# Degree count of a graph kernel: 98-wide high one-hots, and the low keys of eight split five to three between VectorE and ScalarE

## The chip, the cores and the metric

The kernel runs on one core of one Trainium2 chip. The metric is the time of one execution on the device, in microseconds, lower being better; the time shown is the median of three runs.

## The reference

Two message-passing layers with a layernorm after each, over 12,500 nodes of 128 features and 200,000 edges whose destinations are sorted. The part that matters here is the first step, the degree of every node (how many edges end in it), which the first layer needs for its edge weights:

```python
src, dst = (edge_index[0], edge_index[1])
mask = (src != dst).astype(x.dtype)
deg = jax.ops.segment_sum(mask, dst, num_segments=N) + 1.0
dinv = deg ** (-0.5)
edge_w = dinv[src] * dinv[dst] * mask
...
h = x @ W1 + b1
h = spmm(h)          # sum over edges of h[src] * edge_w, by dst
...
```

The second layer is an attention over the same edges with eight heads. None of the rest is touched by the change.

## The kernel before

Node number n is split in two: its node tile (n >> 7, of which there are NT = 98) is the high key, its row in the tile (n & 127) the low key. The 200,000 edges lie as 128 partitions (P) by 1568 columns. A stage is a block in which each engine runs its own instruction list, with semaphores between them; the stages run one after another. The order is: load of keys and constants, `count_destinations`, `find_bases`, then the first layer and so on.

`count_destinations` (the class `Degrees`) makes a table of 98 node tiles by 128 rows out of matmuls. For one column of 128 edges, the one-hot of the high key (an edge per partition, a node tile per column) is the stationary operand, and a row of the low key is the moving one, so that the product adds each edge to its cell. PSUM (`bank[0]` and `bank[1]`) accumulates over all 1568 columns. The columns are taken in halves of HALF = 8; two halves make a turn of TURN = 16, and there are 98 turns, so 196 halves. Per half:

- GpSimd (`stage`) copies the eight columns of both keys in three small copies: two to bf16 (L401), one in f32 (L402). It has four half-sized buffers and may run that far ahead.
- VectorE (`vector_half`) writes `highs` for all eight columns in one `tensor_tensor` (L408): 128 rows by 8 keys, 1024 elements per partition. Then it writes `lows` for the keys of `BY_VECTOR`, four of the eight, in a second one (L411): 128 rows by 4 keys, 512 elements.
- ScalarE (`scalar_half`) makes the other four, `BY_SCALAR`, one `activation` each (L418): the sign of (row + 0.5 - key), 128 elements. The sign form is a running count that the next stage differences again.
- TensorE (`tensor_half`) runs eight matmuls of 128 stationary by 129 moving columns (the last one counts all edges): four with `lows` into `bank[1]` (L430), four with `signs` into `bank[0]` (L434).

`highs`, `lows` and `signs` each have two half-sized buffers: VectorE and ScalarE may write a half once TensorE has used the half two before it. In SBUF `highs` is laid out [row, key], the key innermost, so that one key's stationary operand is read at a step of 8 elements (16 bytes); one key's `lows` are read at a step of 4 elements (8 bytes); `signs` are contiguous. A second class, `CountUpto`, does a like count beside the first layer; its one-hots are 98 wide and have 8 keys innermost, and its matmul is L518:

```python
self.highs = tmp("highs", [P, 2, NT, HALF], BF16)
self.upto = tmp("upto", [P, 2, P, HALF], BF16)
...
counted = nc.tensor.matmul(bank[0][0:NT, 0:P], self.highs[:, h, :, j], self.upto[:, h, :, j], start=False, stop=False)
```

In a profile the stationary operand's load stands as LDWEIGHTS on PEld and the product as MATMUL on PE. L778, L788 and L808 are matmuls of the second layer's sort that the rows below show; L808 moves `hot_hi`, 98 columns at a step of 16 bytes, L778 and L788 move contiguous bf16.

Of the kernel before, what the change touches and what calls it, by code (L numbers as in the profile page):

```python
# [5 lines left out]
F32, I32, BF16, U16 = mybir.dt.float32, mybir.dt.int32, mybir.dt.bfloat16, mybir.dt.uint16  # L6
ALU, ACT, AX = mybir.AluOpType, mybir.ActivationFunctionType, mybir.AxisListType

P = 128
# [3 lines left out]
NT = -(-N_NODES // P)  # L13
LAST_ROWS = N_NODES - (NT - 1) * P
PAD_NODE = NT * P - 1
HALF = 8
# [40 lines left out]
def need(eng, sem, value):  # L57

    if isinstance(value, int) and value <= 0:
        return  # L60
    eng.wait_ge(sem, value)
# [31 lines left out]
def gnn(nc, x, src, dst, attr, w1, b1, w2, b2, gamma, beta, bn_mean, bn_var,  # L93
# [14 lines left out]
    with whole:  # L108
        def sb(name, shape, dt=F32):
            return whole.enter_context(nc.sbuf_tensor(name, shape, dt))  # L110

        bank = [whole.enter_context(nc.psum_tensor(f"bank{i}", [P, 512], F32)) for i in range(8)]
# [5 lines left out]
        iota_rows = sb("iota_rows", [P, P, HALF], BF16)  # L118
# [6 lines left out]
        zeros_bf = sb("zeros_bf", [P, P + 1], BF16)  # L125
# [86 lines left out]
        with ExitStack() as ph:  # L212
            sem = ph.enter_context(phase_semaphores(nc))
            tmp = lambda n, s, d=F32: ph.enter_context(nc.sbuf_tensor(n, s, d))
# [160 lines left out]
        class Degrees:  # L375


            BY_VECTOR, BY_SCALAR = (0, 1, 2, 3), (4, 5, 6, 7)

            def __init__(self, sem, tmp):  # L380
                self.highs_ready, self.lows_ready, self.signs_ready, self.used, self.keys_ready, self.ones_ready, self.go = (
                    sem(n) for n in ("highs_ready", "lows_ready", "signs_ready", "hot_used", "keys_ready", "ones_ready", "go"))
                by_vector, by_scalar = len(self.BY_VECTOR), len(self.BY_SCALAR)
                self.highs = tmp("highs", [P, 2, P, HALF], BF16)
                self.lows = tmp("lows", [P, 2, P + 2, by_vector], BF16)
                self.signs = tmp("signs", [P, 2, by_scalar, P + 2], BF16)
                self.keys_bf, self.keys = tmp("keys_bf", [P, 4, 2, HALF], BF16), tmp("keys", [P, 4, HALF])
# [16 lines left out]
            def vector_half(self, dve, i, b, h):  # L404
                v = nc.vector
                need(dve, self.used, (i - 1) * TURN + (h + 1) * HALF)
                dve.wait_ge(self.keys_ready, (2 * i + h + 1) * 3)
                v.tensor_tensor(self.highs[:, h, :, :], iota_rows[:, :, :], self.keys_bf[:, 2 * b + h, 0, :].unsqueeze(1).to_broadcast([P, P, HALF]),  # L408
                                ALU.is_equal).then_inc(self.highs_ready, 1)
                some = len(self.BY_VECTOR)  # L410
                v.tensor_tensor(self.lows[:, h, 0:P, :], iota_rows[:, :, 0:some], self.keys_bf[:, 2 * b + h, 1, 0:some].unsqueeze(1).to_broadcast([P, P, some]),  # L411
                                ALU.is_equal).then_inc(self.lows_ready, 1)
# [7 lines left out]
            def zeros(self, **at):  # L420

                for n in range(2):
                    nc.tensor.matmul(bank[n][:, 0:P + 1], zeros_bf[:, 0:P], zeros_bf[:, :], **at)

            def tensor_half(self, pe, i, h):
                half = 2 * i + h
                pe.wait_ge(self.highs_ready, half + 1)
                pe.wait_ge(self.lows_ready, half + 1)
                for j in self.BY_VECTOR:
                    nc.tensor.matmul(bank[1][:, 0:P + 1], self.highs[:, h, :, j], self.lows[:, h, 0:P + 1, j],  # L430
                                     start=False, stop=False).then_inc(self.used, 1)
                for n, j in enumerate(self.BY_SCALAR):
                    pe.wait_ge(self.signs_ready, half * len(self.BY_SCALAR) + n + 1)
                    nc.tensor.matmul(bank[0][:, 0:P + 1], self.highs[:, h, :, j], self.signs[:, h, n, 0:P + 1],  # L434
                                     start=False, stop=False).then_inc(self.used, 1)

        class Count:
# [1309 lines left out]
        with ExitStack() as ph:  # L1747
            own = ph.enter_context(phase_semaphores(nc))
            sem = lambda n: own(f"qkv_{n}")
            tmp = lambda n, s, d=F32: ph.enter_context(nc.sbuf_tensor(f"qkv_{n}", s, d))  # L1750
# [104 lines left out]
        with ExitStack() as ph:  # L1855
            own = ph.enter_context(phase_semaphores(nc))
            sem = lambda n: own(f"expand_{n}")
            tmp = lambda n, s, d=F32: ph.enter_context(nc.sbuf_tensor(f"expand_{n}", s, d))
# [143 lines left out]
        with ExitStack() as ph:  # L2002
            own = ph.enter_context(phase_semaphores(nc))
            sem = lambda n: own(f"score_{n}")
            tmp = lambda n, s, d=F32: ph.enter_context(nc.sbuf_tensor(f"score_{n}", s, d))
# [226 lines left out]
        with ExitStack() as ph:  # L2232
            own = ph.enter_context(phase_semaphores(nc))
            sem = lambda n: own(f"soft_{n}")
            tmp = lambda n, s, d=F32: ph.enter_context(nc.sbuf_tensor(f"soft_{n}", s, d))
# [6 lines left out]
            BY_VECTOR = CHUNK_LEN * 3 // 4  # L2242
# [62 lines left out]
        with ExitStack() as ph:  # L2305
            own = ph.enter_context(phase_semaphores(nc))
            sem = lambda n: own(f"mix_{n}")
            tmp = lambda n, s, d=F32: ph.enter_context(nc.sbuf_tensor(f"mix_{n}", s, d))
# [143 lines left out]
        with ExitStack() as ph:  # L2452
            own = ph.enter_context(phase_semaphores(nc))
            sem = lambda n: own(f"fin_{n}")
            tmp = lambda n, s, d=F32: ph.enter_context(nc.sbuf_tensor(f"fin_{n}", s, d))
# [112 lines left out]
```

## Time and profile before

| what | value |
|---|---|
| median of 3 runs | 9340.04 us |
| lowest and highest | 9331.43, 9343.38 us |
| the profiled execution: time | 9334.91 us |
| the profiled execution: span | 9333.3 us |
| granted TensorE clock, mean | 0.796 of full |
| `count_destinations` in that span | about 51 to 284 us |

The span is from the first to the last instruction of the one profiled execution; the 1.6 us between span and time lie outside it. The stage that the change touches is 2.5% of the span, so a tenth of its length is 0.25% of the time. Busy time is the union of an engine's instructions; where instructions of one engine overlap, as ScalarE's and TensorE's do, the mean duration of one is longer than the time that each adds.

### The profile page before, as it was taken

Reading aid. Unit: us, or ns where it says so; the run is one execution under the profiler, and the core shown is the slowest. Engines: PE = TensorE matmul, PEld = TensorE weight load, DVE = VectorE, ACT = ScalarE, POOL = GpSimd, SP = SyncE. Lnnn points to the kernel's source line nnn. Section 1 sums busy time; section 2 is a strip of 40 time slices with the busy share of each in tenths; the row PEclk is TensorE's granted clock in tenths of the full one; section 3 lists DMA queues with packets and bytes.
Section 4 is the critical chain, followed back from the end, with each engine's and each line's share of the span. In section 5 each row is a group of like instructions: output and inputs, shape, how many; then the busy total and the mean of one; then the engine's idle time right before and its main releaser. Section 6 shows DMA issues by size and latency. Waiting matters only on the chain. (4 is left out here: it accounts for less than half of the span.)

```text
span 9333.3 us, 196145 instructions
## 1 busy us (share of the span) xinstructions
PE 6708.6 (72%) x37588; PEld 5384.7 (58%) x37589; DVE 5772.2 (62%) x15905; ACT 2627.6 (28%) x9043; POOL 6065.1 (65%) x6650
## 2 busy tenths in 40 slices
PE   6688888888677777777777646666666658854774
PEld 5556565656466766666666524444444447754663
DVE  7544444445466666666666565555555558888887
ACT  7311111111223333333333110000000025535884
POOL 6477777777655555555555657777777767744665
PEclk8688888898667677767677677878878789987997
DMA  1233333344321111111111133333333356643663
GB/s 45 57 105 107 107 106 108 108 110 109 94 75 42 42 42 42 42 41 41 40 40 39 46 98 114 114 113 114 114 113 114 114 156 167 168 107 103 165 164 96
DMA packets 1043673, 868.47 MB, mean 93 GB/s; under 512 B 188168, under 2 KB 936312, under 8 KB 1043624
## 3 DMA queue, kind: packets, MB, share of 16 engines
q0 software_dynamic: 179664, 437.87, 15.3%
q1 hardware_dynamic: 643032, 319.49, 13.1%
q10 hardware_dynamic: 220928, 110.57, 4.1%
q8 instruction: 16, 0.26, 0.0%
q14 instruction: 33, 0.27, 0.0%
HBM read 578.04 MB, written 287.84 MB: 93 GB/s over the span
## 5 line engine op out<-in xcount | busy, mean ns | idle before, releaser
L1561 POOL DMA_INDIRECT spmm_rows<-h_table,spmm_index_ring x3136 | 3120.1, 995 | 1738.7 <-issue 862.8
L1640 PE MATMUL bank<-spmm_rows,spmm_hot 128*128 x6660 | 1808.6, 365 | 145.5 <-SPq L1536 94.8
L1919 POOL DMA_INDIRECT kv_sorted<-expand_payload,expand_where_ring x1568 | 1503.5, 959 | 498.4 <-issue 398.3
L1640 PEld LDWEIGHTS bank<-spmm_rows,spmm_hot 128*128 128x128 f32 x6660 | 1404.2, 253 | 584.3 <-issue 564.2
L1612 DVE TENSOR_TENSOR region_ab<-region_ab,bank 128x128 f32 x3330 | 957.0, 287 | 1204.8 <-PE bank L1640 808.4
L1940 PE MATMUL bank<-region_ab,expand_hot_t 128*128 x3336 | 1117.2, 493 | 733.7 <-DVE expand_hot_t L1957 732.9
L1974 DVE SCALAR_TENSOR_TENSOR expand_payload<-expand_payload,region_c,bank 128x256 f32 x1668 | 801.1, 480 | 878.4 <-SPq L1881 620.2
L1940 PEld LDWEIGHTS bank<-region_ab,expand_hot_t 128*128 128x128 f32 x3336 | 765.5, 240 | 942.7 <-issue 817.1
L845 ACT COPY spmm_beside_next_slot<-bank 128x98 f32<-128x98 f32 x1568 | 377.6, 241 | 1903.3 <-PE bank L808 1895.8
L808 PE MATMUL bank<-spmm_beside_hot_hi,spmm_beside_hot_lo 128*128 128x98 bf16 x1568 | 556.3, 355 | 481.6 <-issue 481.6
L518 PE MATMUL bank<-spmm_beside_upto,spmm_beside_highs 128*98 128x128 bf16 x1568 | 686.3, 438 | 254.8 <-issue 252.0
L816 PE MATMUL bank<-spmm_beside_next_slot,spmm_beside_lo_t 128*128 128x98 f32 x3136 | 833.9, 361 | 0.0
L816 PEld LDWEIGHTS bank<-spmm_beside_next_slot,spmm_beside_lo_t 128*128 128x128 f32 x3136 | 738.3, 282 | 28.4
L767 DVE CUSTOM_DVE_ANT_0 spmm_beside_junk<-bank,spmm_beside_hot_hi 128x98 f32<-128x98 f32 x1568 | 450.2, 324 | 485.9 <-PE bank L817 485.9
L2111 POOL TENSOR_TENSOR score_terms<-score_q_sb,score_k_rows 128x512 f32<-128x512 f32 x420 | 528.8, 1269 | 240.0 <-ACT score_q_sb L2059 207.3
L2443 PE MATMUL bank<-mix_mixed,mix_hot 128*128 128x136 f32 x3360 | 489.6, 298 | 174.3 <-DVE region_ab L2407 161.9
L640 ACT COPY spmm_beside_attr_t<-bank 128x512 f32<-128x512 f32 x392 | 229.4, 585 | 1343.1 <-PE bank L679 1340.8
L1591 DVE TENSOR_TENSOR spmm_hot<-iota_bf,lo_slots 128x512 f32<-128x512 bf16 x834 | 576.9, 692 | 20.5 <-issue 20.5
L2346 POOL TENSOR_TENSOR mix_mixed<-mix_mixed 128x512 f32<-128x512 f32 x420 | 436.4, 1060 | 233.2 <-ACT mix_mixed L2361 152.0
L2443 PEld LDWEIGHTS bank<-mix_mixed,mix_hot 128*128 128x128 f32 x3360 | 437.7, 190 | 227.9 <-DVE region_ab L2407 200.7
L518 PEld LDWEIGHTS bank<-spmm_beside_upto,spmm_beside_highs 128*98 128x98 bf16 x1568 | 407.0, 260 | 274.7 <-issue 271.3
L817 PE MATMUL bank<-spmm_beside_hot_hi,spmm_beside_earlier 128*128 128x98 bf16 x1568 | 550.0, 351 | 0.0
(358 smaller groups left out, 11797.0 us busy)
## 6 DMA issues: line engine op xcount, KB each, us to landing
score_k_rows<-kv_sorted SPq DMA_DIRECT2D x420, 288.0 KB
mix_mixed<-kv_sorted SPq DMA_DIRECT2D x420, 256.0 KB
spmm_beside_attr_sb<-in_edge_attr_dram ACTq DMA_DIRECT2D x390, 256.0 KB
spmm_rows<-h_table,spmm_index_ring POOLq DMA_INDIRECT x3136
kv_sorted<-expand_payload,expand_where_ring POOLq DMA_INDIRECT x1568
kv_sorted<-spmm_beside_blank SPq DMA_DIRECT2D x1, 15232.0 KB
kv_sorted<-spmm_beside_blank SPq DMA_DIRECT2D x98, 136.0 KB
h_table<-region_ab SPq DMA_DIRECT2D x28, 448.0 KB, 3.0
```

What stands on the lines that cost most here:

```text
L518: counted = nc.tensor.matmul(bank[0][0:NT, 0:P], self.highs[:, h, :, j], self.upto[:, h, :, j], start=False, stop=False)
L808: t.matmul(self.running[:, 0:NT], self.hot(self.hot_lo, k, P), high, start=False, stop=True, skip_group_check=True).then_inc(self.counted, 1)
L816: t.matmul(self.found_at(k), self.lo_t[:, k // 2 % self.PAIRS, at], self.next_slot[:, k % self.NEXTS, :], start=True, stop=False)
L817: last = t.matmul(self.found_at(k), self.earlier[:, k // 2 % 2, at], high, start=False, stop=True)
L1561: nc.gpsimd.indirect_dma_start(rows[:, k, :], None, table, bass.IndirectOffsetOnAxis(ap=index_ring[:, h, k % HALF:k % HALF + 1], axis=0)). ...
L1591: nc.vector.tensor_tensor(hot[:, b % HOT_GROUPS, :, :], iota_bf[:, :].unsqueeze(1).to_broadcast([P, HOTS, P]), lo_slots[:, bass.ds(g * HOT ...
L1612: nc.vector.tensor_tensor(here, here, sums_of(m), ALU.add).then_inc(added, 1)
L1640: last = nc.tensor.matmul(sums_of(k), hot[:, k // HOTS % HOT_GROUPS, k % HOTS, :], tile_of(rows, place[k % HALF]), start=True, stop=True)
L1919: nc.gpsimd.indirect_dma_start(kv_sorted, bass.IndirectOffsetOnAxis(ap=where_ring[:, h, k % HALF:k % HALF + 1], axis=0), payload[:, k, 0:R ...
L1940: last = nc.tensor.matmul(into, hot_t[:, j % 2, m * P:(m + 1) * P], tile_of(kv_nodes, node[m]), start=True, stop=True)
L1974: v.scalar_tensor_tensor(here, here, same_window[:, bass.ds(t, 1)], made_here, ALU.mult, ALU.add).then_inc(joined, 1)
L2443: last = nc.tensor.matmul(bank[k % RING][:, stream * W:(stream + 1) * W], hot[:, b, c, :], mixed[:, b, c, :], start=True, stop=True)
```

## The change

`highs` gets 98 rows in place of 128, so L408 compares with `iota_rows[:, 0:NT, :]` and writes 784 elements in place of 1024, and both kinds of matmul have a stationary operand of 98 columns and write 98 PSUM partitions. VectorE takes five of the eight low keys and ScalarE three: `lows` is [P, 2, 130, 5] in place of [P, 2, 130, 4], L411 writes 640 elements, and a key's `lows` are read at a step of 5 elements (10 bytes).

```diff
-            BY_VECTOR, BY_SCALAR = (0, 1, 2, 3), (4, 5, 6, 7)
+            BY_VECTOR, BY_SCALAR = (0, 1, 2, 3, 4), (5, 6, 7)
...
-                self.highs = tmp("highs", [P, 2, P, HALF], BF16)
+                self.highs = tmp("highs", [P, 2, NT, HALF], BF16)
...
-                v.tensor_tensor(self.highs[:, h, :, :], iota_rows[:, :, :], self.keys_bf[:, 2 * b + h, 0, :].unsqueeze(1).to_broadcast([P, P, HALF]),
+                v.tensor_tensor(self.highs[:, h, :, :], iota_rows[:, 0:NT, :], self.keys_bf[:, 2 * b + h, 0, :].unsqueeze(1).to_broadcast([P, NT, HALF]),
...
             def zeros(self, **at):
                 for n in range(2):
-                    nc.tensor.matmul(bank[n][:, 0:P + 1], zeros_bf[:, 0:P], zeros_bf[:, :], **at)
+                    nc.tensor.matmul(bank[n][0:NT, 0:P + 1], zeros_bf[:, 0:NT], zeros_bf[:, :], **at)
...
-                    nc.tensor.matmul(bank[1][:, 0:P + 1], self.highs[:, h, :, j], self.lows[:, h, 0:P + 1, j],
+                    nc.tensor.matmul(bank[1][0:NT, 0:P + 1], self.highs[:, h, :, j], self.lows[:, h, 0:P + 1, j],
...
-                    nc.tensor.matmul(bank[0][:, 0:P + 1], self.highs[:, h, :, j], self.signs[:, h, n, 0:P + 1],
+                    nc.tensor.matmul(bank[0][0:NT, 0:P + 1], self.highs[:, h, :, j], self.signs[:, h, n, 0:P + 1],
```

## Rows read from the trace of the kernel before

**Rows 1.** Windows: length; busy us (count) of PE, PEld, DVE, ACT, POOL; clock, DMA share, GB/s.

```profile
51.00:284.00 233.00, 195.68 (x1570) 166.19 (x1570) 198.97 (x392) 231.70 (x784) 166.14 (x586) 0.78 0.10 28
284.00:364.00 80.00, 24.55 (x79) 17.48 (x79) 36.19 (x64) 2.19 (x5) 16.09 (x17) 0.52 0.09 22
```

**Rows 2.** Groups of instructions within 51:284: busy us, mean ns of one | idle before.

```profile
L418 ACT ACTIVATE count_d_signs<-iota_half,count_d_keys 128x128 bf16<-128x128 bf16 x784 | 231.7, 390 | 10.3 <-POOL count_d_keys L402 10.3
L408 DVE TENSOR_TENSOR count_d_highs<-iota_rows,count_d_keys_bf 128x1024 bf16<-128x1024 bf16 x196 | 136.5, 696 | 34.0 <-POOL count_d_keys_bf L401 11.9 <-PE bank L434 7.6 <-POOL count_d_keys L402 6.6
...
L401 POOL CAST count_d_keys_bf<-region_ab 128x8 bf16 x384 | 103.9, 301 | 62.0 <-ACT count_d_signs L418 44.8 <-DVE count_d_highs L408 12.2 <-DVE count_d_lows L411 2.8
...
L411 DVE TENSOR_TENSOR count_d_lows<-iota_rows,count_d_keys_bf 128x512 bf16<-128x512 bf16 x196 | 81.7, 417 | 0.0
...
L402 POOL COPY count_d_keys<-region_ab 128x8 f32 x192 | 72.2, 376 | 0.0
```

**Rows 3.** Waits within 51:284: who waited for whom, us, times, longest.

```profile
POOL count_d_keys_bf L401 <- ACT count_d_signs L418: 44.8, 103, 0.7
PEld bank L430 <- DVE count_d_highs L408: 41.1, 76, 1.6
PE bank L430 <- DVE count_d_lows L411: 34.4, 100, 1.4
```

**Rows 4.** L408 by itself: durations, first and last start.

```profile
L408 DVE TENSOR_TENSOR count_d_highs<-iota_rows,count_d_keys_bf x196: 678/693/739, 51.1 to 281.4; 128x1024 bf16<-128x1024 bf16 x196
```

**Rows 5.** Windows of 20 us at full and at half clock, columns as in rows 1.

```profile
64.00:84.00 20.00, 16.62 (x139) 14.21 (x139) 17.87 (x36) 20.00 (x69) 13.75 (x53) 1.00 0.55 151
...
264.00:284.00 20.00, 17.64 (x133) 14.20 (x130) 15.93 (x32) 18.78 (x63) 10.42 (x39) 0.50 0.00 0
```

**Rows 6.** Timeline, VectorE: start us, us, then the instruction.

```profile
150.83 0.42 DVE L411 TENSOR_TENSOR count_d_lows<-iota_rows,count_d_keys_bf 128x512 bf16<-128x512 bf16 x1
151.22 0.69 DVE L408 TENSOR_TENSOR count_d_highs<-iota_rows,count_d_keys_bf 128x1024 bf16<-128x1024 bf16 x1
151.83 0.42 DVE L411 TENSOR_TENSOR count_d_lows<-iota_rows,count_d_keys_bf 128x512 bf16<-128x512 bf16 x1
```

**Rows 7.** Timeline, TensorE's matmuls of one half, four and four.

```profile
60.50 0.66 PE L430 MATMUL bank<-count_d_lows,count_d_highs 128*128 128x129 bf16 x4
60.98 0.61 PE L434 MATMUL bank<-count_d_signs,count_d_highs 128*128 128x129 bf16 x4
```

**Rows 8.** Lines L430, L434 and L518: duration ns min/median/max of weight load and matmul.

```profile
L430 PEld LDWEIGHTS bank<-count_d_lows,count_d_highs x784: 141/147/175, 52.2 to 282.8; 128*128 128x128 bf16 x196
L430 PE MATMUL bank<-count_d_lows,count_d_highs x784: 289/302/315, 52.3 to 282.9; 128*128 128x129 bf16 x196
...
L434 PE MATMUL bank<-count_d_signs,count_d_highs x784: 220/288/319, 52.7 to 283.3; 128*128 128x129 bf16 x196
...
L518 PEld LDWEIGHTS bank<-spmm_beside_upto,spmm_beside_highs x1568: 253/255/283, 424.2 to 2351.5; 128*98 128x98 bf16 x196
```

**Rows 9.** Timeline, weight loads around L518 in the first layer.

```profile
601.99 0.26 PEld L518 LDWEIGHTS bank<-spmm_beside_upto,spmm_beside_highs 128*98 128x98 bf16 x1
602.14 0.42 PEld L1640 LDWEIGHTS bank<-spmm_rows,spmm_hot 128*128 128x128 f32 x2
```

**Rows 10.** Timeline, matmuls of the same stretch.

```profile
602.09 0.43 PE L518 MATMUL bank<-spmm_beside_upto,spmm_beside_highs 128*98 128x128 bf16 x1
602.35 0.40 PE L1640 MATMUL bank<-spmm_rows,spmm_hot 128*128 x2
```

**Rows 11.** Timeline, matmuls in the second layer.

```profile
4001.20 0.28 PE L778 MATMUL bank<-ident_bf,spmm_beside_hot_lo 128*128 128x128 bf16 x2
4001.33 0.33 PE L808 MATMUL bank<-spmm_beside_hot_hi,spmm_beside_hot_lo 128*128 128x98 bf16 x1
4001.48 0.38 PE L816 MATMUL bank<-spmm_beside_next_slot,spmm_beside_lo_t 128*128 128x98 f32 x2
```

## The prediction

> **What bounds the kernel now.** I first cut the span into windows around the stage [rows 1]. The reader is to see that from 51 to 284 us ScalarE is busy for 231.7 of 233 us, while VectorE (199.0), TensorE (195.7) and GpSimd (166.1) all have slack. After the stage ScalarE is nearly idle: nothing there waits for more than the end of this stage, so a microsecond taken from or added to the stage is one of the whole time. The groups of the stage [rows 2] give the length of the work: 784 activations in 231.7 us, 0.2955 us each (390 ns is one's own duration; neighbours overlap), four per half, 1.18 us. The first and last start of L408 agree: 195 steps from 51.1 to 281.4 us are 1.181 us per half [rows 4]. So the stage is 196 x 1.181 = 231.5 us, and its period is ScalarE's.
>
> The waits [rows 3] show who is late behind ScalarE: GpSimd waits for its signs before it restages keys, and TensorE waits for VectorE's highs and lows, 75 us in all. TensorE is not the bound, and its load and matmul have room. The granted clock matters little: at clock 1.00 it does 139 matmuls in 20 us, at 0.50 it does 133 [rows 5].
>
> **The change part by part.**
>
> *ScalarE* loses one activation in four: 3 x 0.2955 = 0.887 us per half, 173.8 us in all. It stops being the bound.
>
> *VectorE.* Start to start, L408 takes 0.61 us and L411 0.39 [rows 6], 1.00 us per half. Their durations, 693 [rows 4] and 417 ns [rows 2], differ by 276 ns for 512 elements, 0.54 ns per element. The step of 0.61 is then 1024 x 0.54 = 0.55 plus 0.06, that of 0.39 is 0.275 plus 0.115. The new L408 has 784 elements: 0.42 + 0.06 = 0.48. The new L411 has 640: 0.345 + 0.115 = 0.46 if the rate holds, so 0.94 us per half. Against that: rows of five bf16 are odd, and none of this trace's VectorE rows has an odd innermost row of bf16. If such rows lose the doubled rate, an element costs 1.07 ns, L411 0.69 + 0.115 = 0.80 and VectorE 1.28 us per half. I take 0.94, since source and destination still step by one inside a row, and keep 1.28 as a bound. The Trainium skill (Vector Engine (DVE) Microarchitecture Reference, 5.1 Performance modes) says that with two sources a pair of 16-bit elements may span two rows of odd length, which speaks for 0.94; no run here shows it.
>
> *TensorE's weight load.* This is where the change can bite. A load of 128 columns read at a 16-byte step lasts 147 ns (L430), a load of 98 columns at the same step 255 ns (L518) [rows 8]. The narrower load is the slower one. What counts is how long the next load is held up. Weight loads stand one behind the other: L518's starts at 601.99 and the next at 602.14, 0.15 to 0.16 us later with rounding [rows 9]; I take 0.158, that is 1.6 ns per column. L518's own matmul is noted as starting at 602.09 and the next one at 602.35 [rows 10], which fits a matmul that streams only once its load is done. A load does run beside the matmul before it, so in a stream of such pairs the step is the longer of the two. For the eight matmuls of a half that is at least 8 x 0.158 = 1.264 us, more than the 1.181 of today.
>
> The Trainium skill (TensorE: Matmul & The Clock Gate, Weight-path perf modes) has a rule against this change: fast weight load is on only when the number of weights is 128 and the type is not fp32. The trace agrees: 147 against 255 ns [rows 8]. [...]
>
> *TensorE's moving operand.* Today L430's four matmuls stand in 0.66 us, so (0.66 - 0.302) / 3 = 0.12 us each at a step of 8 bytes; L434's contiguous ones (0.61 - 0.288) / 3 = 0.107 [rows 7, 8]. At a 16-byte step L808 needs 4001.48 - 4001.33 = 0.155 for 98 columns, 1.6 ns per column, where contiguous L778 needs 0.065 [rows 11]. So the step costs. A key's lows will lie 10 bytes apart. If each 16 bytes passed cost 1.6 ns, 8 bytes would give 129 x 0.8 = 0.103 (0.12 measured) and 10 bytes 0.129, scaled by the same ratio 0.15. That is still beneath the weight load. The far bound is the 16-byte price, 129 x 1.6 = 0.206, or 0.26 as L518 to its follower shows in rows 10, less what that follower's own wider load adds; I take 0.235 as the upper bound. The lower one is 0.12, hidden. My value for the five lows matmuls is 0.165, a little over the load, as today's 0.12 is a little over 0.107; the three signs ones (0.107) take the load's 0.158.
>
> *The rest, each at nothing.* GpSimd's three copies per half are unchanged; (103.9 + 72.2) / 196 = 0.90 us per half at most [rows 2], hidden beneath TensorE. If that cover went, VectorE would wait for keys and 0.90 us would be the floor of a half. The two `zeros` pairs, once each, change by less than 0.1 us. No DMA and no queue is touched. The next stage reads rows 0 to 97 of both banks as it did; Its clock is low already (0.52 in rows 1), so it loses nothing.
>
> *What is late next.* With TensorE the bound, VectorE (0.94) and ScalarE (0.89) run up to two halves ahead and then wait for a free buffer, so that TensorE's own waits fall to the start of the stage.
>
> *The sum.* TensorE per half: 3 x 0.158 + 5 x 0.165 = 1.299 us. Times 196 this is 254.6 us; less 231.5 it is +23.1. On the profiled execution's own 9334.9 that gives 9358.0; the median of the three runs lies 5.1 above it, so on the runs' scale 9363. The bounds: all eight at 0.158, 247.7 us, +16 (9356). The lows at 0.235: 3 x 0.158 + 5 x 0.235 = 1.649, 323.2 us, +92 (9432).
>
> **The rivals.**
>
> *A, faster: the 98-wide load hides.* If the 0.158 is peculiar to L518's surroundings (its follower there is an f32 matmul with a longer load), a half is bound by VectorE: 0.94, or about 1.0 with GpSimd's 0.90 so near. 196 x 1.0 = 196 us, -35: 9305. It decides from a weight-load step below 1.181 / 8 = 0.148 us on. For it: today's load at 128 columns does hide. Against it: 255 ns against 147 for the same layout.
>
> *B, much slower: the 10-byte step reads like the 16-byte one.* The five lows matmuls take 0.206 to 0.235 each, the half 1.50 to 1.65: +63 to +92, 9403 to 9432. For it: L808's and L518's rows; against it: 8 bytes cost next to nothing, and 10 is nearer.
>
> *C, the odd row of five halves VectorE's rate.* VectorE then needs 1.28, TensorE 1.30: two nearly equal engines with two buffers between them give perhaps 1.31 to 1.40, an estimate. That is +25 to +43: 9365 to 9383.
>
> *D, no change.* TensorE's load at 0.148 to 0.158 with no loss at the half's start: 1.18 to 1.27 us, 0 to +18, 9340 to 9358. This is the low end of my own case rather than another mechanism, but it falls on the other side of what a measurement can tell.
>
> **How the numbers follow.** A measurement of this kernel can tell about 0.2%, 18.7 us, from no change. The chances: my case at 1.276 us per half or more 0.40, D 0.20, B 0.16, C 0.12, A 0.12. The likeliest gives 9363, its own range 9356 to 9385. The range for 8 in 10 leaves out A and little else: 9345 to 9430. Faster by over 0.2%: A, 0.12. Within 0.2%: D and a little of C's low end, 0.22. Slower: the rest, 0.66.
>
> **What would show it.** In the changed profile: L418 x588 with gaps before it and ScalarE near 75% of the stage; PEld busy nearly throughout with loads of about 255 ns at L430 and L434, and loads 0.158 us apart; the waits that end with VectorE or ScalarE waiting for TensorE's matmuls, and few the other way; the stage about 255 us long; 784 elements at about 564 ns in L408 and 640 at about 487 in L411. Loads of 147 ns would make A right. L430 matmuls 0.2 us apart would make B right. L411 near 830 ns, with TensorE still waiting for it, would make C right. Any move of time outside the stage would make the whole sum wrong.

## The result, and the profile after

The changed kernel takes 9402.48 us (median of 4 runs, 9397.73 to 9407.8) against 9339.88 us before (4 runs): ratio 1.0069, 95% interval 1.0051 to 1.0086, so it is slower by 62.6 us. The forecast was 9363, slower, with a range to 9430. The direction and the range held; the size did not: 62.6 us is outside the likeliest case's own range (9356 to 9385).

The durations by line in the changed kernel, as in [rows 8] and [rows 4] (min/median/max ns, then first and last start in us):

```profile
L430 PEld LDWEIGHTS bank<-count_d_lows,count_d_highs x980: 253/276/278, 53.4 to 348.0; 128*98 128x98 bf16 x196
L430 PE MATMUL bank<-count_d_lows,count_d_highs x980: 358/360/434, 53.4 to 348.2; 128*98 128x129 bf16 x196
...
L434 PEld LDWEIGHTS bank<-count_d_signs,count_d_highs x588: 276/276/277, 54.2 to 348.6; 128*98 128x98 bf16 x196
L434 PE MATMUL bank<-count_d_signs,count_d_highs x588: 341/387/388, 54.4 to 348.7; 128*98 128x129 bf16 x196
...
L408 DVE TENSOR_TENSOR count_d_highs<-iota_rows,count_d_keys_bf x196: 566/568/596, 52.2 to 346.2; 128x784 bf16<-128x784 bf16 x196
...
L411 DVE TENSOR_TENSOR count_d_lows<-iota_rows,count_d_keys_bf x196: 545/552/556, 52.7 to 346.7; 128x640 bf16<-128x640 bf16 x196
```

The weight loads of the stage now last 276 ns (median) where they lasted 147, and they do so whether the matmul moves lows at 10 bytes (L430) or contiguous signs (L434). L408's starts give (346.2 - 52.2) / 195 = 1.508 us per half, against 1.181. The stage ends at 348.7 + 0.39 = 349.1 us; before it ended at 283.6. What follows takes 9396.2 - 349.1 = 9047.1 us of the span, before 9333.3 - 283.6 = 9049.7. So the loss lies wholly in the stage: 196 x (1.508 - 1.181) = 64 us.

The windows of the stage and of everything behind it, columns as in [rows 1]:

```profile
51.00:350.00 299.00, 296.32 (x1572) 289.99 (x1572) 203.18 (x392) 193.49 (x588) 187.84 (x591) 1.00 0.08 21
...
350.00:9396.00 9046.00, 6497.63 (x36007) 5198.36 (x36007) 5548.04 (x15473) 2394.01 (x8257) 5911.59 (x6036) 0.80 0.33 95
```

TensorE is now busy for 296 of 299 us and its loads for 290; ScalarE fell to 193.5. The granted clock rose to 1.00 for the whole stage from 0.78, and the stage is slower all the same: this is not a matter of the clock. The waits turned round, as the forecast had it (who waited for whom, us, times, longest, within 51:345):

```profile
ACT count_d_signs L418 <- PE bank L434: 100.9, 193, 0.8
DVE count_d_highs L408 <- PE bank L434: 89.0, 189, 0.7
```

A timeline of the changed kernel, some lines of 200 to 206 us, in order of time:

```profile
201.11 0.97 PEld L430 LDWEIGHTS bank<-count_d_lows,count_d_highs 128*98 128x98 bf16 x5
...
201.99 0.64 PEld L434 LDWEIGHTS bank<-count_d_signs,count_d_highs 128*98 128x98 bf16 x3
202.11 0.70 PE L434 MATMUL bank<-count_d_signs,count_d_highs 128*98 128x129 bf16 x3
202.53 1.00 PEld L430 LDWEIGHTS bank<-count_d_lows,count_d_highs 128*98 128x98 bf16 x5
...
202.97 0.57 DVE L408 TENSOR_TENSOR count_d_highs<-iota_rows,count_d_keys_bf 128x784 bf16<-128x784 bf16 x1 [0.57 <-PE bank L434]
203.43 0.64 PEld L434 LDWEIGHTS bank<-count_d_signs,count_d_highs 128*98 128x98 bf16 x3
203.46 0.55 DVE L411 TENSOR_TENSOR count_d_lows<-iota_rows,count_d_keys_bf 128x640 bf16<-128x640 bf16 x1
...
204.12 0.97 PEld L430 LDWEIGHTS bank<-count_d_lows,count_d_highs 128*98 128x98 bf16 x5
```

Two things are to be seen. The three L434 loads span 0.64 us, so they start (0.64 - 0.276) / 2 = 0.18 us apart. And there is a loop through both engines. The half whose first load starts at 201.11 has its last matmul out at 202.11 + 0.70 = 202.81, 1.70 us on. VectorE may write that buffer only then: after 0.57 us of waiting its highs start at 202.97, 0.16 us later, and its two instructions take 1.04 us, to 204.01. The first load of the half that they feed starts at 204.12, 0.11 us later. With two buffers this loop, 1.70 + 0.16 + 1.04 + 0.11 = 3.01 us, is passed once for every two halves: 1.505 us per half, where 1.508 was measured. Sixteen loads alone are 16 x 0.18 = 2.88, 1.44 per half. Both are close, and the longer one sets the pace. The table of waits hides this: a load lasts 0.276 us but starts 0.18 us after the one before, so the load at 204.12 is 0.15 us late and PEld stands idle for only 0.05 us ahead of it.

### The profile page after: what moved, and what is told of

It reads as the page before. It is cut to its first block and busy times, and to the rows that moved or that the text cites. A ratio compares the mean times of both kernels' runs of the same rounds, so it can differ in the third digit from the quotient of the medians.

```text
span 9396.2 us, 195753 instructions
## 1 busy us (share of the span) xinstructions
PE 6796.4 (72%) x37588; PEld 5490.3 (58%) x37589; DVE 5775.1 (61%) x15905; ACT 2589.1 (28%) x8847; POOL 6105.4 (65%) x6650
## 5 line engine op out<-in xcount | busy, mean ns | idle before, releaser
L518 PE MATMUL bank<-spmm_beside_upto,spmm_beside_highs 128*98 128x128 bf16 x1568 | 686.4, 438 | 251.0 <-issue 248.0
L518 PEld LDWEIGHTS bank<-spmm_beside_upto,spmm_beside_highs 128*98 128x98 bf16 x1568 | 407.3, 260 | 271.9 <-issue 268.6
```

## The experiments

The first four runs and the last two were on chips on which the kernel before itself takes 10,746 and 10,633 us. The difference lies behind the counting stage: in e2_split_only what follows the stage takes 10,449 us of the span, and in the first profile of the kernel before 9,050. The counting stage itself hardly differs: the kernel before's own count, inside the run e4_measured below, starts its halves (280.8 - 51.9) / 195 = 1.174 us apart, against 1.181; that is 1.4 us of stage between two profiles of the same code. So the stage's own period is compared throughout, and the time only as a ratio to runs of the kernel before on the same chip.

| run | loads, split, buffers | us per half | stage against before, 196 halves | time against before (95% interval) |
|---|---|---|---|---|
| before | 128, 4/4, 2 | 1.181 | | |
| after | 98, 5/3, 2 | 1.508 | +64 | 1.0069 (1.0051 to 1.0086) |
| e1_98_only | 98, 4/4, 2 | 1.442 | +51 | 1.004 (1.0025 to 1.0054) |
| e2_split_only | 128, 5/3, 2 | 1.358 | +35 | 1.0032 (1.0021 to 1.0043) |
| e3_pad_5_3 | 128 (98 compared), 5/3, 2 | 1.303 | +24 | 1.0026 (1.0016 to 1.0035) |
| e5_pad_4_4 | 128 (98 compared), 4/4, 2 | 1.169 | -2 | 1.0 (0.999 to 1.0009) |
| e7_unrolled | after, half as many loop ends | 1.508 | +64 | 1.0066 (1.0051 to 1.0081) |
| e8_pad_5_3_four | 128 (98 compared), 5/3, 4 | 1.118 | -12 | 0.9986 (0.9977 to 0.9995) |
| e9_before_four | 128, 4/4, 4 | 1.169 | -2 | 0.9998 (0.9988 to 1.0007) |
| e10_after_four | 98, 5/3, 4 | 1.44 | +51 | 1.0043 (1.0027 to 1.0058) |
| e11_pad_four_turn_keys | e8 with keys staged by the turn | 0.991 | -37 | 0.9965 (0.9953 to 0.9978) |

The period is (last - first start of the highs instruction) / 195. In e10 VectorE runs ahead, so it is taken from TensorE's signs matmuls there, (334.7 - 0.36 - 53.2) / 195, where 0.36 are the two steps from the first to the last of a half's three. In e9 it also runs ahead, and the period is that before less 2.4 us / 196, by which the stage's end moved (283.6 to 281.2). The runs with four buffers also have TensorE's loop over two turns in place of one, for the buffers' addresses; e7 shows that this alone changes nothing.

### One half of the change at a time

e1_98_only is the changed kernel with the old split:

```diff
-            BY_VECTOR, BY_SCALAR = (0, 1, 2, 3, 4), (5, 6, 7)
+            BY_VECTOR, BY_SCALAR = (0, 1, 2, 3), (4, 5, 6, 7)
```

> The narrow highs alone, keys split four and four as before, so lows are read at 8 bytes. Theory W (a 98-column weight load holds every matmul to 0.180 us, whatever it moves): the half stays at 1.51 us, the stage near 295 us, the time near 9402 (+63). Theory M (the 10-byte step of the lows is what costs): the five slow matmuls are gone, the half falls to the 1.18 us of ScalarE, the time to about 9340.

Measured: 1.442 us per half, from (332.4 - 51.3) / 195. The narrow loads alone cost 51 us of stage, and the lows at 8 bytes did not help them: theory M falls. The figure is 8 x 0.180 to within 2 ns, so here TensorE's stream of loads is the bound and nothing else. It is also 0.066 below the changed kernel, which W as written (295 us) did not foresee. The durations, as above:

```profile
L408 DVE TENSOR_TENSOR count_d_highs<-iota_rows,count_d_keys_bf x196: 566/567/579, 51.3 to 332.4; 128x784 bf16<-128x784 bf16 x196
...
L434 PEld LDWEIGHTS bank<-count_d_signs,count_d_highs x784: 276/276/277, 53.0 to 334.7; 128*98 128x98 bf16 x196
```

e2_split_only is the kernel before with the new split:

```diff
-            BY_VECTOR, BY_SCALAR = (0, 1, 2, 3), (4, 5, 6, 7)
+            BY_VECTOR, BY_SCALAR = (0, 1, 2, 3, 4), (5, 6, 7)
```

> The split five to three alone, highs 128 wide. Theory W: loads of about 147 ns come back, TensorE needs about 0.9 to 1.0 us per half, and VectorE sets the pace with 0.61 + 0.52 = 1.13 us (0.52 is L411's new 552 ns less the overlap it had): 221 us, 10 below before, 9330. Theory M: the 10-byte step keeps a lows matmul at 0.180 or more and the half at 1.2 us or more: 9345 or more.

Measured: 1.358 us per half, slower than before by 35 us, though its weight loads are back at 145 ns. Both theories were wrong about it: no engine has 1.36 us of work in a half (VectorE 0.61 + 0.52, ScalarE 0.88, TensorE and GpSimd about 1.07 each). This is what brought up the loop of the section above. In this run's trace (load at 201.95, last matmul out at 203.23, highs at 203.39, lows done at 204.55, load at 204.67) the loop is 1.28 + 0.16 + 1.16 + 0.12 = 2.72 us, or 1.36 per half.

e3_pad_5_3 keeps the 128-row tile, so the loads stay 128 wide, but compares only 98 rows:

```diff
-                v.tensor_tensor(self.highs[:, h, :, :], iota_rows[:, :, :], self.keys_bf[:, 2 * b + h, 0, :].unsqueeze(1).to_broadcast([P, P, HALF]),
+                v.tensor_tensor(self.highs[:, h, 0:NT, :], iota_rows[:, 0:NT, :], self.keys_bf[:, 2 * b + h, 0, :].unsqueeze(1).to_broadcast([P, NT, HALF]),
...
+                nc.gpsimd.memset(self.highs[:, :, NT:P, :], 0.0).then_inc(self.ones_ready, 1)
```

> The highs tile keeps 128 rows, VectorE fills only the first 98 and GpSimd zeroes the last 30 once, so that every weight load has 128 columns; split five to three. The sums in rows 98 to 127 are then zero and never read. Theory W: VectorE needs 0.48 + 0.52 = 1.00 us per half, TensorE 0.9 to 1.05: 196 to 206 us for the stage, 25 to 35 below before, 9305 to 9315. Theory M: no better than 9345.

Measured: 1.303, a miss for the same reason. Against e2 only VectorE's first instruction changed, by 0.125 us (691 to 569 ns), and the half by 0.055, about half of it: an instruction inside a loop that is passed once in two halves counts by half. Some lines of its timeline, in order of time:

```profile
199.90 0.62 PEld L431 LDWEIGHTS bank<-count_d_lows,count_d_highs 128*128 128x128 bf16 x5 [0.52 <-DVE count_d_highs L409]
199.93 0.93 PE L431 MATMUL bank<-count_d_lows,count_d_highs 128*128 128x129 bf16 x5 [0.30 <-DVE count_d_lows L412]
...
200.68 0.51 PE L435 MATMUL bank<-count_d_signs,count_d_highs 128*128 128x129 bf16 x3
200.92 0.18 POOL L403 COPY count_d_keys<-region_ab 128x8 f32 x1
...
201.35 0.58 DVE L409 TENSOR_TENSOR count_d_highs<-iota_rows,count_d_keys_bf 128x784 bf16<-128x784 bf16 x1 [0.54 <-PE bank L431]
201.45 0.53 POOL L403 COPY count_d_keys<-region_ab 128x8 f32 x1
...
201.85 0.55 DVE L412 TENSOR_TENSOR count_d_lows<-iota_rows,count_d_keys_bf 128x640 bf16<-128x640 bf16 x1
...
202.51 0.62 PEld L431 LDWEIGHTS bank<-count_d_lows,count_d_highs 128*128 128x128 bf16 x5 [0.53 <-DVE count_d_highs L409]
```

TensorE's half goes from its first load at 199.90 to its last matmul's end at 201.19, 1.29 us. VectorE has waited 0.54 us and starts 0.16 later, takes 1.05 to 202.40, and 0.11 after that the first load of the half that it feeds starts, at 202.51. In all 1.29 + 0.16 + 1.05 + 0.11 = 2.61 us for two halves, 1.305 each, against 1.303. TensorE waited for VectorE and VectorE for TensorE, and neither was full.

### The disputed cost by itself

e4_measured adds to the kernel before, behind its count, 48 matmuls each of twelve forms (into a spare bank) and eight `tensor_tensor` each of nine forms.

```diff
+                for _ in range(48):
+                    nc.tensor.matmul(bank[2][0:98, 0:128], self.highs[:, 0, 0:98, 0], self.signs[:, 0, 0, 0:128], start=True, stop=True)
...
+                for _ in range(8):
+                    v.tensor_tensor(out(5), iota_rows[:, :, 0:5], key(5), ALU.is_equal).then_inc(self.measured, 1)
```

> The kernel before with extra work behind the count: twelve groups of 48 matmuls each into a spare bank, with stationary operands of 128, 127, 98 and 64 columns at a 16-byte step and of 128 and 98 contiguous columns, and moving ones contiguous and at 8, 10, 12 and 16 bytes; and nine groups of eight tensor_tensor each, with rows of 3 to 7 bf16. Its results are thrown away and its time only says how long they take. Theory W: steps of about 0.055 to 0.11 us at 128 columns and a contiguous moving operand, 0.18 at 98 and also at 127 (the count of 128 is what matters, not how many fewer), 0.12 at 64 (1.6 ns per column plus 20); contiguous 98 columns lie well below 0.18. Theory M: the 10-byte step alone gives 0.18 at 128 columns. VectorE: rows of five take as long as rows of six (about 550 ns) if each row ends on its own tick, and about 480 if pairs span rows; the row that is padded in only one operand tells which one matters.

The groups by line: shape, count, busy us, mean ns of one. The stationary operands `count_d_highs` are read at 16 bytes, `zeros_bf` contiguously; L443, L445, L447 and L449 move theirs at 8, 10, 12 and 16 bytes, the others contiguously:

```profile
L449 PE MATMUL bank<-iota_rows,count_d_highs 128*128 128x128 bf16 x48 | 11.4, 414 | 0.0
L435 PE MATMUL bank<-count_d_signs,count_d_highs 128*127 128x128 bf16 x48 | 11.4, 437 | 0.0
...
L433 PE MATMUL bank<-count_d_signs,count_d_highs 128*98 128x128 bf16 x48 | 8.8, 361 | 0.0
L447 PE MATMUL bank<-iota_rows,count_d_highs 128*128 128x128 bf16 x48 | 8.7, 359 | 0.0
...
L445 PE MATMUL bank<-iota_rows,count_d_highs 128*128 128x128 bf16 x48 | 7.4, 331 | 0.0
...
L443 PE MATMUL bank<-count_d_lows,count_d_highs 128*128 128x128 bf16 x48 | 6.0, 301 | 0.0
...
L437 PE MATMUL bank<-count_d_signs,count_d_highs 128*64 128x128 bf16 x48 | 6.0, 321 | 0.0
...
L469 DVE TENSOR_TENSOR count_d_scratch<-iota_rows,count_d_keys_bf 128x640 bf16<-128x640 bf16 x8 | 4.5, 559 | 0.3
L481 DVE TENSOR_TENSOR count_d_scratch<-iota_rows,count_d_keys_bf 128x768 bf16<-128x768 bf16 x8 | 4.5, 558 | 0.3
L465 DVE TENSOR_TENSOR count_d_scratch<-iota_rows,count_d_keys_bf 128x640 bf16<-128x640 bf16 x8 | 4.5, 558 | 0.3
...
L477 DVE TENSOR_TENSOR count_d_scratch<-iota_rows 128x640 bf16<-128x640 bf16 x8 | 3.9, 492 | 0.3
L431 PE MATMUL bank<-count_d_signs,count_d_highs 128*128 128x128 bf16 x48 | 3.8, 253 | 0.0
...
L439 PE MATMUL bank<-count_d_signs,zeros_bf 128*128 128x128 bf16 x48 | 2.9, 219 | 0.0
L441 PE MATMUL bank<-count_d_signs,zeros_bf 128*98 128x128 bf16 x48 | 2.8, 219 | 0.0
```

The step from one matmul to the next is (busy - one) / 47. At a 16-byte step of the stationary operand it is 0.121 us for 64 columns, 0.180 for 98, 0.233 for 127, and 0.075 for 128: some 1.8 ns per column, and at exactly 128 it drops. Contiguous 98 columns take 0.055, like contiguous 128 at 0.057. So it is neither the width nor the step alone, but a width other than 128 with a step.

The groups did not all run at one granted clock, so two of them are taken apart: L431 (128 columns) and L433 (98), first the clock of four windows (columns as in [rows 1]), then the timelines within them.

```profile
283.10:284.30 1.20, 1.20 (x14) 1.20 (x13) 1.10 (x3) 0.00 (x0) 0.00 (x0) 0.50 0.00 0
285.00:286.70 1.70, 1.70 (x32) 1.70 (x31) 1.60 (x4) 0.00 (x0) 0.00 (x0) 1.00 0.00 0
287.00:291.00 4.00, 4.00 (x24) 4.00 (x24) 3.76 (x8) 0.00 (x0) 0.00 (x0) 1.00 0.00 0
292.00:295.00 3.00, 3.00 (x18) 3.00 (x18) 2.83 (x6) 0.00 (x0) 0.00 (x0) 0.50 0.00 0
```

```profile
283.09 1.06 PE L431 MATMUL bank<-count_d_signs,count_d_highs 128*128 128x128 bf16 x8
284.79 1.99 PE L431 MATMUL bank<-count_d_signs,count_d_highs 128*128 128x128 bf16 x30
286.83 4.42 PEld L433 LDWEIGHTS bank<-count_d_signs,count_d_highs 128*98 128x98 bf16 x24
291.87 3.34 PEld L433 LDWEIGHTS bank<-count_d_signs,count_d_highs 128*98 128x98 bf16 x18
```

At 128 columns the step is (1.06 - 0.31) / 7 = 0.107 us at the lower level of the clock (0.50) and (1.99 - 0.22) / 29 = 0.061 at the upper (1.00); the 0.075 above mixes the two. At 98 columns it is 0.180 at both: (4.42 - 0.276) / 23 and (3.34 - 0.276) / 17. The 127 columns ran at 0.50 throughout. So at like clocks 98 columns cost three times what 128 cost at 1.00 (0.180 against 0.061), and 127 twice as much at 0.50 (0.233 against 0.107); and 128 columns at a 16-byte step cost about what contiguous ones do (0.061 against 0.057, both at 1.00).

With 128 columns loaded, the moving operand costs 0.121 at 8 bytes, 0.150 at 10, 0.177 at 12 and 0.234 at 16. That is about a constant price per byte passed, which refutes rival B's price for 10 bytes. The 12 and 16 bytes ran at a clock of 0.50, the 8 at 1.00 and the 10 at 0.88 in the mean; at 1.00 the 10-byte step is the same, (0.93 - 0.329) / 4 = 0.150 by e3's five lows matmuls above (0.329 us is the median of one). W's guesses held in order and for 98, 64 and the cliff at 128; for 127 the guess of 0.18 was too low.

For VectorE, rows of five (L465) last as long as rows of six (L481), 558 ns, also where the first source's rows touch (L469). Only with both sources and the output dense do 640 elements take 492 (L477), which is the rate the forecast had used.

### Where the last 13 us come from

e7_unrolled is the changed kernel with TensorE's loop over two turns:

> The changed kernel with TensorE's loop over two turns in place of one, so half as many loop ends. If the 0.13 us beyond 16 x 0.180 that each turn takes is the refill of TensorE's queue after a branch, the stage falls by 49 x 0.13 = 6.5 us, from 297 to 290. If it comes from the five to three split itself (the order of waits within a half), it stays at 297.

```diff
-                    with pe.Fori(0, E_TURNS) as i:
-                        for h in range(2):
-                            work.tensor_half(pe, i, h)
+                    with pe.Fori(0, E_TURNS // 2) as m:
+                        for b in range(2):
+                            for h in range(2):
+                                work.tensor_half(pe, m * 2 + b, h)
```

Measured: 1.508, unchanged; the loop's end costs nothing here. The time that stood at the loop's end in the trace, as a later start of the first load, was a wait for the lows.

e10_after_four gives the changed kernel four buffers, a half's index 2 * b + h in place of h, and lets VectorE and ScalarE wait for the use two turns back:

```diff
-                need(dve, self.used, (i - 1) * TURN + (h + 1) * HALF)
+                need(dve, self.used, (i - 2) * TURN + (h + 1) * HALF)
...
-                self.highs = tmp("highs", [P, 2, NT, HALF], BF16)
+                self.highs = tmp("highs", [P, 4, NT, HALF], BF16)
```

> The changed kernel (98-column loads, five to three) with four buffers in place of two. Theory R (of its 3.015 us per turn, 2.88 are sixteen weight loads and the rest is the two-buffer round trip): 16 x 0.180 = 2.88, 282 us of stage, 13 below the changed kernel, the time near 9385. If the rest is anything in TensorE's own stream, it stays at 295.

Measured: 1.44 us per half, 8 x 0.180. The time is 1.0043 of before where the changed kernel had 1.0069, but their intervals overlap, so that the periods carry this and not the times. So of the changed kernel's 1.508, 1.44 is the loads and 0.068, 13 us in all, the two-buffer loop. With e1 (same loads, VectorE's pass 0.13 us shorter, also 1.44) the two agree.

If the same loop took part in the kernel before, e5_pad_4_4 (the edit of e3 with the old split) and e9_before_four (four buffers) would shorten it in different ways:

> Tile of 128 rows of which 98 are compared, keys four and four, two buffers as before. Theory R (with two buffers a turn is one pass of VectorE, a hand-over, one pass of TensorE to its last result and a hand-over back): VectorE's pass falls from 1.03 to 0.90 us, so ScalarE's 1.18 is left as the bound, 1.17 to 1.18 us per half, no change to before within 3 us of stage. Rival: the narrower compare is worth its own 0.125 us per half, 207 us of stage.

> The kernel before with four buffers in place of two, nothing else. If ScalarE's 0.2955 x 4 = 1.18 us is its bound, as the prediction has it, the stage stays at 231 us within 2. If the two-buffer round trip took part in its 1.181 us, it falls to ScalarE's bare step of 0.2925 x 4 = 1.17, 229 us; more than 4 us below before would mean that ScalarE was not the bound.

Both measure 1.169, less than before by 0.012 us per half or 2.4 us of stage, and down at ScalarE's own 4 x 0.293, from (280.5 - 51.1) / 783 = 0.293 between the starts of e9's activations. Two profiles of the kernel before differ by 1.4 us themselves, so whether the loop cost it anything is not shown. ScalarE was its bound to within 3 us; neither gain can be told in the time. So 98 compared rows are worth nothing by themselves, and neither are four buffers.

### A version that beats both

e8_pad_5_3_four joins e3 (98 rows compared, 128 loaded, split five to three) with the four buffers of e10.

> 128-column loads, 98 rows compared, split five to three, and four buffers of highs, lows and signs in place of two (TensorE's loop over two turns, for the addresses). Theory R: the two-buffer round trip of 1.04 + 0.11 + 1.35 + 0.1 = 2.6 us for two halves, which made 1.30 us per half of the same kernel with two buffers, is gone, and the slowest engine is left: 1.05 to 1.12 us, 206 to 220 us of stage, 12 to 26 below before. Rival (VectorE and GpSimd hold each other up, or the keys come late): 1.2 us or more, no gain over before.

Measured: 1.118 us per half, the stage 12 us shorter, the time 0.9986 (0.9977 to 0.9995). Against e3's 1.303 it confirms the loop. But VectorE's two steps are 1.00 us, so something else is left. Its timelines, GpSimd and then VectorE:

```profile
200.63 0.53 POOL L403 COPY count_d_keys<-region_ab 128x8 f32 x1
201.10 0.71 POOL L402 CAST count_d_keys_bf<-region_ab 128x8 bf16 x2
201.75 0.53 POOL L403 COPY count_d_keys<-region_ab 128x8 f32 x1
```

```profile
201.19 0.57 DVE L409 TENSOR_TENSOR count_d_highs<-iota_rows,count_d_keys_bf 128x784 bf16<-128x784 bf16 x1
201.67 0.55 DVE L412 TENSOR_TENSOR count_d_lows<-iota_rows,count_d_keys_bf 128x640 bf16<-128x640 bf16 x1
202.31 0.57 DVE L409 TENSOR_TENSOR count_d_highs<-iota_rows,count_d_keys_bf 128x784 bf16<-128x784 bf16 x1
```

GpSimd's three copies stand back to back and fill 201.75 - 200.63 = 1.12 us, the whole half. The f32 copy ends at 201.16 and VectorE starts at 201.19. The copies are of eight elements each, yet the f32 one lasts 0.53 us. In e3's timeline above the same copy (L403) lasts 0.18 us at 200.92, where VectorE stands idle, and 0.53 at 201.45, where it works. So the copy is held up beside VectorE, and here VectorE then waits for it. e11_pad_four_turn_keys copies 16 columns at a time:

```diff
-                cols = bass.ds(i * TURN + h * HALF, HALF)
...
+                    some = keys[:, bass.ds(i * TURN, TURN)].rearrange("p (h k) -> p h k", h=2)
+                    nc.gpsimd.tensor_copy(self.keys_bf[:, both, n, :], some).then_inc(self.keys_ready, 1)
```

> As the version with 128-column loads, 98 rows compared, five to three and four buffers, but GpSimd copies the keys of a whole turn at once, three copies of 128 x 16 per turn in place of six of 128 x 8. Theory: in that version GpSimd's copies stand back to back (0.52 + 0.47 + 0.125 = 1.12 us per half), each held up while VectorE works, and both other engines start 0.03 us after the last of them; with half as many, VectorE's 1.00 or TensorE's 1.05 is left, 1.02 to 1.08 us per half, 200 to 212 us of stage, 20 to 30 below before, 9305 to 9315. Rival: something in VectorE or TensorE sets the 1.118: no change.

Measured: 0.991 us per half, from (245.6 - 52.3) / 195, 37 us of stage less than before and a time of 0.9965 (0.9953 to 0.9978), the medians on that chip lying 33 us apart. The rival falls: GpSimd's copies were the bound, for nothing else of the work changed. It is a little better than expected, at VectorE's own 1.00. The window shows TensorE busy for 99% and VectorE for 97% of it, ScalarE for 91% and GpSimd for only 67% (columns as in [rows 1]):

```profile
52.00:248.00 196.00, 193.97 (x1570) 184.16 (x1570) 190.01 (x392) 177.72 (x588) 131.12 (x293) 1.00 0.12 33
```

## Why the prediction was right and wrong

**The bound before: right.** ScalarE's activations set it, to within 0.012 us per half (e9, e5). One reading beside it was off: the 75 us of TensorE's waits count the same stretches twice, once for the loads (41.1) and once for the matmuls (34.4). TensorE's matmuls stood idle for 233 - 195.7 = 37 us. Nothing hung on it.

**The 98-column load becomes the bound: right, and shown.** e1 and e10 stand at eight loads per half whatever the split. The Trainium skill's rule (TensorE: Matmul & The Clock Gate, Weight-path perf modes) that fast weight load needs exactly 128 weights agrees with the drop from 0.233 us at 127 columns to 0.107 at 128, both at a granted clock of 0.50. It is not the whole story, since contiguous 98 columns take 0.055.

**The size of a load's step: too small.** The term that was mis-sized is 3 x 0.158 + 5 x 0.165 = 1.299 us. It measured 8 x 0.180 = 1.440. The 0.158 was the time for which one load held up the next where a single such load stood between others (0.15, or 0.14 to 0.16 with rounding, in [rows 9]); in a row of them the step is 0.02 us more. The 0.165 for the lows came from no row of its own; their matmuls take the load's 0.180 too. That is 0.141 x 196 = 27.6 us.

**"What is late next": wrong, and the step that failed.** The prediction let VectorE and ScalarE "run up to two halves ahead". With two buffers they cannot: a buffer is free only when the last matmul's result is out, and the next half of the same buffer then needs 1.04 us of VectorE. The prediction put TensorE's waits after the start of the stage at nothing; the loop of 3.01 us per two halves was longer than 2.88 us of loads. Its price is (1.508 - 1.440) x 196 = 13.3 us. The three terms, 23.1 + 27.6 + 13.3 = 64.0, are the whole loss.

**The odd row of five: half right.** It did not lose the doubled rate (1.28 us), but L411 lasts 552 ns and not 487: a row of five costs what a row of six costs. The Trainium skill's sentence (Vector Engine (DVE) Microarchitecture Reference, 5.1) that a pair may span two rows of odd length is not what these runs show; 5-wide rows took the time of 6-wide ones (L465, L481) unless all three operands were dense (L477). The prediction held this harmless, beneath TensorE. Being a part of the loop it was not: by the loop's sum it costs an estimated half of 0.065 us per half, which no run isolates.

**The moving operand at 10 bytes: right.** 0.15 us estimated and 0.150 measured, hidden beneath 0.180.

**The rivals.** The time landed at the low edge of B's band (+63 to +92), and B's mechanism is false: e1 keeps 51 of the 64 us of loss without a 10-byte step. A number at a rival's band is no evidence for the rival. A (the load hides) is refuted; C's 1.28 did not happen; D (no change) falls with the 62.6 us. The direction was right for the reason given. That the stated range held the time is in part luck: the prediction's own case ended at 9385, and above that only B and the moving operand's upper bound, both wrong, reached to 9430.

**A split that looked free.** The prediction counted the move of a key as 0.3 us off ScalarE. e2 shows that the split alone costs 35 us: it lengthens VectorE's pass (L411 from 418 to 552 ns) and TensorE's (five lows at 0.150 in place of four at 0.121), and both lie in the loop.

## What to carry to other kernels

Two engines that hand buffers to and fro with two buffers form a loop: add up one's pass to its last result, the hand-over, the other's pass and the hand-over back, and halve the sum. If that is above the busiest engine's work, moving work between engines gains nothing and more buffers do. Trimming a bf16 stationary operand that is read at a step below the full 128 columns can cost more than it saves, as it did here at 16 bytes: keep the load at 128, zero the spare columns once, and trim only what the other engine computes. And once a bound is lifted look for the small helper (here GpSimd's copies of eight elements), which may be next.

## What the runs showed that I had not expected

- A bf16 stationary operand at a 16-byte step: 0.061 us per matmul at 128 columns and 0.180 at 98 at a granted clock of 1.00; 0.107 at 128, 0.180 at 98 and 0.233 at 127 at 0.50; contiguous, 0.055 at 98 columns and 1.00.
- A bf16 moving operand of 128 columns with 128-column loads: 0.121, 0.150, 0.177 and 0.234 us at steps of 8, 10, 12 and 16 bytes.
- VectorE's `tensor_tensor` in bf16: rows of five and of six both last 558 ns for 128 rows.
- GpSimd's f32 copy of 128 x 8 in e3: 0.18 us where VectorE is idle, 0.53 beside its two-source instructions.
- The stage ran slower at a granted clock of 1.00 than before at 0.78: the step of a 98-column load at 16 bytes is 0.180 us at either level of the clock.
